# A gate's clamps on GpSimd instead of VectorE, its inflow scale as a scaled copy on ScalarE

## The reference, cut to what matters

```
ek  = exp(min(f, 30))
num = forward(ek*f) + backward(ek*f) - ek*f + exp(min(u+f, 30))*f
den = forward(ek)   + backward(ek)   - ek   + exp(min(u+f, 30))
gate = sigmoid(x) * num / max(den, 1e-8) * (0.8 + 0.2*tf)
```

## Time and profile before

| | |
|---|---|
| median of 3 runs (lowest, highest) | 2559.3 us (2554.54, 2562.68) |
| profiled execution, span from the first to the last instruction | 2556.7 us |
| busy PE / PEld | 2296.2 us (90%) / 1704.1 us (67%) |
| busy DVE | 1875.4 us (73%) |
| busy ACT / POOL | 944.4 us (37%) / 683.5 us (27%) |
| the 120 clamp instructions of VectorE (L440, L441) | 89.9 us |

### The profile page before, as it was taken

How to read it: one execution, slowest core, us unless ns; L and a number is a source line. 1 busy time by engine, 2 the same in 40 slices (tenths; PEclk the granted TensorE clock), 3 DMA queues, 4 the chain that set the end, 5 groups by cost and what they waited for, 6 DMA issues and landing times.

```text
span 2556.7 us, 34018 instructions
## 1 busy us (share of the span) xinstructions
PE 2296.2 (90%) x10567; PEld 1704.1 (67%) x10568; DVE 1875.4 (73%) x2875; ACT 944.4 (37%) x1956; POOL 683.5 (27%) x545
## 2 busy tenths in 40 slices
PE   0789989999898899899878999999999988999998
PEld 0345444454455678778666888888888876788886
DVE  8989898989896765676545668768777785666665
ACT  3243342342432232342343444444534444322222
POOL 5434434343341443335331012122212210000000
PEclk9999999999997899999988999999999998999999
DMA  5000001010023432343241000010010101000001
GB/s 207 17 33 33 33 17 50 17 43 23 33 83 130 144 115 82 114 149 115 99 160 34 1 33 17 17 38 21 17 38 21 49 17 50 25 25 25 25 12 66
DMA packets 50503, 142.21 MB, mean 56 GB/s; under 512 B 4768, under 2 KB 4768, under 8 KB 46064
## 3 DMA queue, kind: packets, MB, share of 16 engines
q1 hardware_dynamic: 31872, 89.89, 10.0%
q10 hardware_dynamic: 12864, 32.81, 3.6%
q0 software_dynamic: 5680, 18.62, 2.4%
HBM read 106.95 MB, written 34.34 MB: 55 GB/s over the span
## 4 chain that ended last, share of the span: by engine, by line
PE 42%; issue 30%; POOL 10%; DVE 8%; POOLq 6%; ACT 3%; DMA 0%; ACTq 0%; DVEq 0%; another core or an unknown queue 0%; SPq 0%
PE bank L341 9%; PE bank L343 9%; PE bank L342 9%; PE bank L2351 3%; PE bank L2352 3%; PE bank L2350 3%; PE bank L2304 3%; POOLq L494 2%; POOL g_v L495 2%; POOL g_v L502 2%; POOLq L517 1%; POOLq L520 1%; POOLq L506 1%; POOL g_eu L501 1%; POOL g_s L516 1%
## 5 line engine op out<-in xcount | busy, mean ns | idle before, releaser
L2179 PE MATMUL bank<-um,w_in 128*128 128x512 f32 x576 | 262.4, 610 | 7.1 <-DVE lm L1515 7.0
L2179 PEld LDWEIGHTS bank<-um,w_in 128*128 128x128 f32 x576 | 109.5, 195 | 138.2 <-issue 125.1
L341 PE MATMUL bank<-u_hi,aw_hi 128*128 (+1 forms) x384 | 158.6, 413 | 12.9 <-DVE u_lo L1920 9.2
L1135 ACT ACTIVATE probs<-bank,nmx 128x128 f32<-128x128 f32 (+3 forms) x256 | 131.7, 528 | 91.6 <-DVE nmx L1943 91.6
L1142 ACT ACTIVATE pt_hi<-bank 128x512 fp32r<-128x512 f32 (+1 forms) x192 | 94.0, 526 | 164.7 <-PE bank L2304 163.5
L343 PE MATMUL bank<-u_hi,aw_lo 128*128 (+1 forms) x384 | 151.9, 395 | 0.0
L342 PE MATMUL bank<-u_lo,aw_hi 128*128 (+1 forms) x384 | 151.8, 395 | 0.0
L1958 DVE TENSOR_TENSOR pt_lo<-bank,pt_hi 128x512 fp32r<-128x512 f32 (+1 forms) x192 | 108.7, 593 | 42.4 <-ACT pt_hi L1142 38.6
L341 PE MATMUL bank<-u_hi,fw_hi 128*128 128x512 f32 x352 | 136.9, 389 | 0.0
L342 PE MATMUL bank<-u_lo,fw_hi 128*128 128x512 f32 x352 | 136.9, 389 | 0.0
L343 PE MATMUL bank<-u_hi,fw_lo 128*128 128x512 f32 x352 | 136.9, 389 | 0.0
(11 more groups left out here) (388 smaller groups left out, 6235.9 us busy)
## 6 DMA issues: line engine op xcount, KB each, us to landing
m_stage<-in_moe SPq DMA_DIRECT2D x21, 1024.0 KB, 5.3
y_slot<-m_o ACTq DMA_DIRECT2D x39, 256.0 KB, 2.7
g_v<-in_fT SPq DMA_DIRECT2D x18, 512.0 KB, 3.5
gates<-g_v SPq DMA_DIRECT2D x18, 512.0 KB, 2.8
f_stage<-in_ffn SPq DMA_DIRECT2D x11, 768.0 KB, 4.3
u_g<-gates SPq DMA_DIRECT2D x8, 1024.0 KB, 9.5
aw_in<-in_att SPq DMA_DIRECT2D x4, 1280.0 KB
w_in<-in_w_in ACTq DMA_DIRECT2D x1, 4640.0 KB, 17.1
```

The costliest lines, as they stand in the source:

```text
L341: nc.tensor.matmul(out, hi_w, hi_x, start=start, stop=False)
L1135: A(probs[:, h % 2, PR_AT[qb]:PR_AT[qb] + w], S_[bk][:, c0:c0 + w], ACT.Exp, bias=nmx[:, h % 2, qb:qb + 1], scale=SCALE, accum_out=rsum[:, ...
L2179: mm = M(dst[:], w_in[:, k, c0:c0 + P], um[:, k, :], start=(k == 0), stop=(k == KC - 1))
```

## The change

For the 60 tiles that are made in pairs:

- VectorE's two clamps go. The semaphore `g_clamped` and the waits on it go with them.
- ScalarE makes, behind the two exponentials of a tile, a third instruction: ek = ek * inflow, a Copy with a scale. It waits for its own first exponential on a new semaphore `g_raw`.
- GpSimd waits for ScalarE (`g_exp`) and makes, ahead of its two products: a copy of one column (the cap exp(30) * inflow of this tile) into `cap`, a drain, min of ek with that column, min of eu with exp(30) (each as a two-step instruction whose second step, max with 0, changes nothing), and a drain.
- A table of caps `ek_max` is made once in the set-up (128x64).

Cut to its core, with the removals of the calls in VectorE's list shown by two of them:

```diff
-            A(ek, v, ACT.Exp).then_inc(g_exp, 1)
+            A(ek, v, ACT.Exp).then_inc(g_raw, 1)
             A(eu, v, ACT.Exp, bias=u_all[:, bass.ds(k * 2 + (G_VEC + t), 1)]).then_inc(g_exp, 1)
-
-        def gate_clamp(eng, k, s, t):
-            _, _, ek, eu = g_tile(s, t)
-            eng.wait_ge(g_exp, k * 4 + (2 * t + 2))
-            nc.vector.tensor_scalar(ek, ek, EXP30, inflow[:, bass.ds(k * 2 + (G_VEC + t), 1)], ALU.min, ALU.mult).then_inc(g_clamped, 1)
-            nc.vector.tensor_scalar(eu, eu, EXP30, None, ALU.min).then_inc(g_clamped, 1)
+            eng.wait_ge(g_raw, k * 2 + (t + 1))
+            A(ek, ek, ACT.Copy, scale=inflow[:, bass.ds(k * 2 + (G_VEC + t), 1)]).then_inc(g_exp, 1)
...
-            eng.wait_ge(g_clamped, k * 4 + (2 * t + 2))
+            eng.wait_ge(g_exp, k * 4 + (2 * t + 2))
+            nc.gpsimd.tensor_copy(cap[:, t:t + 1], ek_max[:, bass.ds(k * 2 + (G_VEC + t), 1)])
+            eng.drain()
+            nc.gpsimd.tensor_scalar(ek, ek, cap[:, t:t + 1], 0.0, ALU.min, ALU.max)
+            nc.gpsimd.tensor_scalar(eu, eu, EXP30, 0.0, ALU.min, ALU.max)
+            eng.drain()
             mult(e, ek, v, ALU.mult)
...
+            setup.inc(V.tensor_scalar(ek_max[:], inflow[:], EXP30, None, ALU.mult))
...
-                clamp(mamba_pair(b, 0), 0)
                 dve.wait_ge(dt_raw, b + 1)
...
-                clamp(mamba_pair(b, 0), 1)
```

More of the change, by code:

```diff
@@ L114, in network @@
         edge = sb("edge", [P, N_GATES * TILES])
+        ek_max = sb("ek_max", [P, N_GATES * TILES])
+        cap = sb("cap", [P, 2])
         gw = sb("gw", [P, KC, E])
@@ L264, in network @@
         g_out = [sem(f"g_out{i}") for i in range(3)]
[L265 removed]
+        g_raw, ob_read = sem("g_raw"), sem("ob_read")
         g_exp, g_vec, g_pool, pre_in = sem("g_exp"), sem("g_vec"), sem("g_pool"), sem("pre_in")
@@ L372, in network @@
         DVE_MAMBA = 67
-        SETUP_STEPS = 23
+        SETUP_STEPS = 24
         PRE_CLAMPED = {(0, 1): SETUP_STEPS + 4, (1, 0): SETUP_STEPS + 7, (1, 1): SETUP_STEPS + 12}
@@ L849, in _ @@
                     A(eu, v, ACT.Exp, bias=u_all[:, 2 * i + t:2 * i + t + 1]).then_inc(setup_act, 1)
+            act.wait_ge(setup_step, SETUP_STEPS)
             for t in range(2):
@@ L1309, in _ @@
             assert setup.n == SETUP_STEPS, setup.n
-            def clamp(pair, t):
-                gate_clamp(dve, *pair, t)
             def scans(pair, t):
@@ L1435, in _ @@
             pre_den_sum(1, 1)
-            clamp((0, 0), 0)
             setup.wait()
@@ L1446, in _ @@
             setup.inc(V.tensor_tensor(d0, r, d0, ALU.mult))
-            clamp((0, 0), 1)
             setup.wait()
@@ L1559, in _ @@
                         inverse(first)
-                    elif q == 6:
-                        clamp(second, 0)
-                        clamp(second, 1)
                     elif q > 6:
@@ L1619, in _ @@
                     V.tensor_tensor(xj[:, P:T], xj[:, P:T], zs[:, j, P:T], ALU.mult).then_inc(y_done, 1)
-                    if j == 0:
-                        clamp(third, 0)
-                    elif j == 1:
+                    if j == 1:
                         forward(third, 0)
-                        clamp(third, 1)
                     elif j == 2:
@@ L1635, in _ @@
                         inverse(third)
-                    elif j == 7:
-                        clamp(fourth, 0)
-                        clamp(fourth, 1)
                 scans(fourth, 0)
@@ L1869, in block_dve @@
                     inverse((k, s))
-                elif (h, q) == (1, 2):
-                    clamp((k + 1, s), 0)
-                    clamp((k + 1, s), 1)
                 more = (q < 1) if last else (h, q) != (1, 2)
@@ L1884, in _ @@
             u_lo_split(1)
-            clamp(moe_pair(0), 0)
-            clamp(moe_pair(0), 1)
             with dve.Fori(0, NBLK // 6) as pair:
@@ L2036, in att_dve @@
                     dense_add(i - 1, 3)
-                if g == 0:
-                    clamp(pair, 0)
-                elif g == 1:
+                if g == 1:
                     gate_backward(dve, *pair, 1, 1)
@@ L2048, in att_dve @@
                     gated_input(1)
-                if g == 0:
-                    clamp(pair, 1)
-                elif g == 1:
+                if g == 1:
                     dens(pair)
```

## The result

The changed kernel takes **2601.4 us** (median of 5 runs, 2598.35 to 2615.42) against 2560.9 us (5 runs) for the kernel before: ratio 1.0172, 95% interval 1.0154 to 1.0190, some 40 us slower. Repeated beside the experiments on two other chips it gave 1.0196 (1.0171 to 1.0221) and 1.0168 (1.0136 to 1.0200). The forecast was 2590, with a range of 2551 to 2632: the sign and the range held, the size came out 10 us short.

The account below looks back on a forecast made before the run. The prediction took TensorE and VectorE to bound the Mamba loop, and TensorE alone the experts and attention. Its terms, 9.3 - 1.5 + 10.6 + 4.8 + 1.3 + 4 + 2 = +30.5 us, gave 2590, range 2551 to 2632.

Parts of the forecast that it names:

- rival A: Whole kernel: GpSimd's one-input clamps don't hold VectorE up, only the relief is left, -18 us, 2541; chance 0.13.
- C: GpSimd's two-step clamp with a column operand costs 1.3 us or more, so the kernel takes 2625 us; chance 0.12.
- three boundaries and chains: dt chains of three Mamba sequences: chain +3.4, start +0.5, taps -0.8 us, together +3.1 each, +9.3 for three.
- first sequence: First Mamba sequence: dt chain starts 3.4 us earlier, lengthens by 2.7, taps 0.8 earlier; sum -1.5.
- `second`, four times: Pair `second`: ScalarE's copies +0.7 us, scans beside the second tile's products +2.0; 2.7 in each of four sequences, +10.6.
- `third`, four times: Pair `third`: forward scans meet the second tile's products, +2.0 us, clamp ahead goes, -0.8; +1.2 four times, +4.8.
- end of the last sequence: End of the last Mamba sequence: VectorE makes um 2.6 us later, 1.3 of it hidden, so +1.3.
- experts: Experts: TensorE's first-trip wait +2.5 us, ScalarE's copies +1, rest 0.5; +4, bounds 0 and +16.
- attention and behind: Attention: normalising step +1.0 us in three steps, row maximum about 1.3 earlier; +2, bounds -1.4 and +6.
- D: One us of GpSimd work costs VectorE a whole us; dt chains gain 6.3 instead of 3.4, 2599 us; chance 0.10.
- start 3.4 earlier: First sequence's dt chain: six clamps ahead go, 4.9 us, new collisions take 1.5, so it starts 3.4 earlier.
- this about pays for the copy: Pair `third`: ScalarE's exponentials start behind GpSimd's output, no longer hit by a clamp, which about offsets ScalarE's copy.

Follow-up runs that it names:

- e_hold: Changed kernel, but GpSimd begins pair `first` of a Mamba sequence only when the dt chain is over: 2609.1 us against 2562.1 before, ratio 1.0188.
- e_eu: Kernel before with one of two clamps moved: GpSimd clamps eu, ek's clamp stays on VectorE: 2559.3 us against 2557.0, ratio 1.0008.
- e_behind: Kernel before with VectorE's clamp of the first tile of `first` moved behind the dt chain: 2554.9 us against 2562.7, ratio 0.9969.
- e_none: Changed kernel without GpSimd's copy and clamps and without ScalarE's scaled copy: 2559.2 us against 2562.1 for the kernel before, ratio 0.9989.
- e_third: Changed kernel run again unedited, on the chip of two other runs: 2598.6 us against 2557.0 for the kernel before, ratio 1.0168.
- e_rest: The change for the 26 tiles beside experts and attention only; the other 34 keep VectorE's clamps: 2568.8 us against 2562.7 before, ratio 1.0022.
- e_again: Changed kernel run again unedited on another chip: 2610.1 us against 2562.7 for the kernel before, ratio 1.0196.
- e_memset: Changed kernel with GpSimd's two clamps of a tile replaced by three settings to zero, which read nothing: 2580.6 us against 2562.1 before, ratio 1.0077.
- e_hold2: Changed kernel with GpSimd's pair `first` held until the dt chain is over, run again unedited: 2591.1 us against 2557.0 before, ratio 1.0117.

## Why the prediction was right, and 10 us short

The sign came from one reading, that GpSimd's work lengthens VectorE's beside it and that clamps in VectorE's list had kept this work out of the dt chain; `e_hold`, `e_eu` and `e_behind` each show the chain follow GpSimd. The lost gate alone makes no loss: `e_none` has a chain of 9.35 us and is no slower than the kernel before. Only with the new work on GpSimd does it cost. The terms of the sum, against TensorE's delay in `e_third` by stage (a boundary runs from a sequence's last pair of heads through the dt chain to the next taps; the measured rows add up to the 38.5 of the table above):

| step | forecast | measured | verdict |
|---|---|---|---|
| relief without collisions (rival A) | -18 | -3 (`e_none`) | A falls: the relief is given back even without new work |
| GpSimd's clamp | 0.7 us | 0.61 and 0.69 free | right; C falls |
| dt chain of the second sequence | 10 us | 11.35 | price mis-sized |
| three boundaries and chains | +9.3 | +15.7 | mis-sized: chain +4.7, not +3.4; no gain at the taps |
| first sequence | -1.5 | +0.4 (profiled +1.8) | failed: the start |
| `second`, four times | +10.6 | +9.3 | sum near, scans +1.3 instead of +2.0 |
| `third`, four times | +4.8 | +6.5 | collision right, copy not paid for |
| end of the last sequence | +1.3 | +2.8 | mis-sized |
| routing | none | +1.4 | left out |
| experts | +4 | +8.4 (`e_rest` with the attention +6) | near the middle of its bounds |
| attention and behind | +2 | -5.9 (profiled -1, `e_again` and `e_rest` +2) | single executions differ by 8 us here |

**The clamp.** Undisturbed, GpSimd's clamp takes 0.61 us with a constant and 0.69 with a column: the 0.7 taken from the nearest row held. The Trainium skill's figure for 512 elements (GPSIMD Engine Reference, section 3.1), 0.77, lay a little above; the measurement decides.

**The price.** The forecast had 0.54 us of VectorE for one of GpSimd, from two chains of the trace before, with gaps of GpSimd counted as work. Its busy time there, 6.00 and 2.45 us, would have given 0.59. The runs give more points: 5.72 us long at 1.63 of GpSimd (`e_hold`), 5.73 at 1.65, 7.57 at 4.11, 9.35 at 6.82, and 11.35 at 9.87 in the changed kernel:

```profile
271.23:282.58 11.35, 6.00 (x14) 2.30 (x13) 10.55 (x18) 3.33 (x6) 9.87 (x12) 0.90 0.26 93
```

From the first to the last this is (11.35 - 5.72) / (9.87 - 1.63) = 0.68, and the three between lie within 0.2 us of that line. Of all 48 chains in the profiles of the kernels without settings, four in each, none lies more than 0.5 us off it; the kernel before, 6.67 at 2.45, lies 0.4 above it. Only `e_memset` lies well under it, at 7.71 for 6.61, by what its settings don't read. So D's whole microsecond is refuted as well.

The chain's term was short on both counts: the price, and GpSimd's work, which grew by 7.4 us (2.45 to 9.87) where the forecast had 6.3. Each boundary cost 5.2 us instead of 3.1, alike in all three of both executions: the start is 0.4 to 0.6 later, as forecast, but the 0.8 us that the taps were to win did not come. This is most of the 10 us that the sum was short.

GpSimd's clamps hold VectorE up too, against the premise of A. In the changed kernel, GpSimd, then VectorE:

```profile
273.61 0.76 POOL L493 TENSOR_SCALAR g_s<-g_s,cap 128x512 f32<-128x512 f32 x1 [0.17 <-issue]
274.44 0.61 POOL L494 TENSOR_SCALAR g_eu<-g_eu 128x512 f32<-128x512 f32 x1
```

```profile
273.85 0.60 DVE L1493 TENSOR_TENSOR dt<-dt 128x64 f32<-128x64 f32 x1
274.48 0.62 DVE L1495 TENSOR_SCALAR dt<-dt 128x64 f32<-128x64 f32 x1
```

Beside the clamps the two take 0.60 and 0.62 us; beside settings the same two took 0.22 and 0.20.

The Trainium skill (SBUF — State Buffer, "Who interferes with whom") says that a VectorE instruction with two inputs in SBUF collides with a GpSimd instruction that reads, not with one that only writes; `e_memset` agrees, 0.22 us beside a setting and 1.17 beside a product.

**The first sequence.** The step that failed is "start 3.4 earlier". The chain began at 89.75 instead of 90.36, 0.6 earlier; in `e_third` and `e_again` it was 1.9. Its length, 11.15, is near the 11.5 forecast. Six clamps were gone from VectorE's list ahead of it, but pair 0's clamps now stand on GpSimd while VectorE makes um and runs pair 0's scans, and GpSimd's own chain got longer. GpSimd and VectorE of the changed kernel there:

```profile
65.65 2.55 POOL L494 TENSOR_SCALAR g_eu<-g_eu 128x512 f32<-128x512 f32 x1
```

```profile
67.65 3.76 DVE L447 TENSOR_TENSOR_SCAN g_s<-decay,g_s 128x512 f32<-128x512 f32 x2
...
86.28 3.35 DVE L482 RECIPROCAL g_s<-g_s 128x512 f32<-128x512 f32 x1 [1.47 <-POOL g_s L511]
```

A clamp took 2.55 us, the scans behind it 3.76, and pair 0's reciprocal began at 86.28, where it had begun at 85.14. So 3 to 4.3 of the 4.9 us were given back, where 1.5 had been put down for collisions.

**`second`.** ScalarE's longer list made TensorE 0.7 us later in each sequence of `e_third`, as forecast for the taps. The scans took 3.65 to 3.72 us in all twelve sequences of the three profiles of the changed kernel, not 4.3. The sign told, a wait for the state products longer by 2 to 3 us, did not come: it is 2.66 where it was 2.41, and the delay came as smaller waits ahead of it (0.57 us for ScalarE and 0.75 for VectorE in the profiled execution). (In the sum, 2.7 four times are 10.8, not 10.6.)

**`third`.** In nine of these twelve sequences the scans took 3.77 us beside the second tile's products: the collision of the forecast, at 1.4 us instead of 2.0. VectorE, then GpSimd, in the second sequence of `e_third`:

```profile
372.70 3.77 DVE L447 TENSOR_TENSOR_SCAN g_s<-decay,g_s 128x512 f32<-128x512 f32 x2
```

```profile
373.40 1.99 POOL L496 TENSOR_TENSOR g_s<-g_s,g_v 128x512 f32<-128x512 f32 x1
```

In the other three, the second sequence of the profiled execution among them, the scans took 2.70, and GpSimd's clamps beside them were the ones held up (1.89 and 1.41 us). With 3.77, TensorE's next pair of heads began 1.4 us later, 8.25 us behind the one before instead of 6.9. Of the three with 2.70, two lost nothing there; the one in the profiled execution lost as much by TensorE's clock, which was granted 0.50 from 373 to 379, where it had been 0.60 from 360.7 to 364.8 and 1.00 behind that. The pair of heads ahead of that also began later. In the second sequence TensorE's wait for ScalarE there is 1.31 us in the profiled execution and 1.75 in `e_third`, where it had been 1.13. VectorE's longer wait for the decay matrix there, 3.53 us instead of 1.65, looks like more than it is: two clamps had stood in its place. VectorE in the kernel before, then ScalarE in the changed kernel:

```profile
353.57 1.49 DVE L440 TENSOR_SCALAR g_s<-g_s,inflow 128x512 f32<-128x512 f32 x1
...
358.12 1.29 DVE L1601 TENSOR_TENSOR lm<-bank,cb 128x512 f32<-128x512 f32 x2 [1.65 <-ACT bank L932]
```

```profile
366.60 0.63 ACT L436 ACTIVATE g_s<-g_v 128x512 f32<-128x512 f32 x1 [4.76 <-POOL g_v L521]
...
367.75 0.71 ACT L439 ACTIVATE g_s<-g_s,inflow 128x512 f32<-128x512 f32 x1
368.37 2.12 ACT L936 ACTIVATE bank<-bank,dt 128x128 f32<-128x128 f32 x8
```

The gate's three instructions stand ahead of the decay matrix, and the first of them waits for GpSimd's output. The step "this about pays for the copy" was wrong by these 0.2 to 0.6 us.

**End and experts.** At `fourth` VectorE waits 9.12 us for the products (in the kernel before 2.65 behind two clamps), and um came 1.7 us later each time, near the 1.3 forecast; at the end of the loop the same delay meets work that had no wait (2.67 us for lm). In the experts TensorE's wait in the first trip rose by the 2.5 us forecast (7.86 against 5.37), but part of it only because TensorE came to it sooner: its delay grew by 1.3 us there in `e_third`. Then the bound's mechanism held in part, second-tile products that reach into scans (4.37 us at 978.71): 1.0 us of TensorE's wait in a later trip, where the bound of +16 has 2 us more for each of six trips.

## What to carry to other kernels

An instruction that looks like load on a busy engine can be the gate that keeps another engine's work out of a tight place: before it is moved, ask what its waiters will do once they are free, and beside what. Where both read SBUF, GpSimd and VectorE did not work as two engines here: count a microsecond of GpSimd's reading beside a chain of small VectorE instructions as some 0.7 us of VectorE (0.68 in these runs), and count the delay of whatever stands behind the added work as well, to which the other half of this loss is put down. The cheap gain was the order: the same clamp, moved behind the chain, gave 0.31%.

## What the runs showed of the hardware

The two engines held each other up in both directions: a clamp of 0.69 us on GpSimd took 2.65 behind scans, and a small VectorE instruction of 0.22 took 1.17 behind a product. Setting memory on GpSimd (0.53 us for 128x512) left VectorE alone: 0.20 to 0.22 us for small instructions beside it, 2.33 for two scans.

TensorE's granted clock was 0.50, the lower of its two levels (1.2 GHz), from 830 to 862 us in the routing of the profiled execution, while TensorE was busy for all 32 us of it. Ahead of it TensorE had waited 5.6 us for ScalarE's copies, which wait for a store. In the kernel before, in `e_third` and in `e_again` the routing has a low stretch too, of 17.1, 13.7 and 13.7 us, behind waits of 2.1 us at most, and the clock rose again while TensorE was busy; in the changed kernel's first profile and in `e_hold` and `e_hold2`, behind waits of 5.5 to 5.6 us, it lasted 34 to 38 us, which cost about 14 us. Why it lasts there, with the engine busy throughout, none of these runs tells apart.
